# Experts' rows weighted on chip and added by scatter to a copy of y in DRAM, residual kept in SBUF, expert weights loaded per tile, experts and combine in one block

## What is computed

```python
h = x; acc = x                                  # x is the layer-normed input
for _ in range(3):
    h = _l2_normalize(_spmm(vals, row, col, h, n_nodes))
    acc = acc + h
x1 = x_in + acc / 4
y = layernorm(x1)
gate_logits = y @ gate_w + gate_b
topk_vals, topk_idx = jax.lax.top_k(gate_logits, 2)
topk_w = softmax(topk_vals)
h = relu(einsum('bsh,ehf->bsef', y, w1) + b1)   # H=256, F=512, E=16
expert_out = einsum('bsef,efh->bseh', h, w2) + b2
z = y + sum(topk_w[..., None] * selected(expert_out))
out = x1 + layernorm(z) * gamma + beta
```

## Time and profile before

| what | us |
|---|---|
| median of 3 runs (lowest, highest) | 1509.21 (1508.99, 1516.28) |
| the profiled execution's own time | 1510.28 |
| its span, first to last instruction | 1508.6 |
| PE busy in the span | 1294.8 (86%) |
| DVE busy | 1113.5 (74%) |
| ACT busy | 883.1 (59%) |
| POOL busy | 248.7 (16%) |

### The profile page before, as it was taken

One profiled execution on the slowest core, in us unless ns is written; L12 is line 12 of the kernel. 1 busy time (PEld: TensorE's weight loads), 2 busy tenths in 40 slices (PEclk: granted clock), 3 DMA queues, 4 the chain that ended last, 5 costly groups with the idle time before them and its releaser, 6 DMA issues. The chain is left out here.

```text
span 1508.6 us, 31442 instructions
## 1 busy us (share of the span) xinstructions
PE 1294.8 (86%) x9378; PEld 1110.7 (74%) x9379; DVE 1113.5 (74%) x1946; ACT 883.1 (59%) x1937; POOL 248.7 (16%) x233
## 2 busy tenths in 40 slices
PE   4588888888799999999999999999977799999800
PEld 1466666767588888888888888888853799999800
DVE  8888989999676656766655766655567688998768
ACT  1678888888755555655555655555341566666522
POOL 1400000000040000000000000000031578887600
PEclk8799999999999999999999999999986899999955
DMA  5088888888886666656666656666322787334384
GB/s 186 28 207 196 201 199 197 203 202 209 216 233 208 184 184 180 194 170 189 182 189 184 190 164 185 178 189 182 113 91 89 238 272 218 108 105 106 89 289 143
DMA packets 225441, 267.36 MB, mean 177 GB/s; under 512 B 15763, under 2 KB 168066, under 8 KB 225298
## 3 DMA queue, kind: packets, MB, share of 16 engines
q1 hardware_dynamic: 211932, 240.41, 58.0%
q0 software_dynamic: 7680, 20.98, 4.8%
q10 hardware_dynamic: 5760, 5.25, 1.4%
HBM read 175.51 MB, written 91.07 MB: 177 GB/s over the span
## 5 line engine op out<-in xcount | busy, mean ns | idle before, releaser
L844 PE MATMUL ps_rows<-h_both,a_high 128*128 (+1 forms) x1875 | 506.2, 398 | 10.5 <-ACT halves L592 5.3
L684 DVE TENSOR_TENSOR a_low<-a_raw,a_high 128x640 fp32r<-128x640 f32 x375 | 305.6, 823 | 233.7 <-ACT a_high L578 230.4
L578 ACT ACTIVATE a_high<-a_raw 128x640 fp32r<-128x640 f32 x375 | 274.6, 740 | 287.6 <-PE ps_rows L847 265.6
L844 PEld LDWEIGHTS ps_rows<-h_both,a_high 128*128 128x128 f32 x1875 | 330.2, 191 | 68.6 <-ACT halves L592 14.4
L847 PEld LDWEIGHTS ps_rows<-h_both,a_low 128*128 128x128 f32 x1875 | 276.1, 191 | 32.9
L847 PE MATMUL ps_rows<-h_both,a_low 128*128 (+1 forms) x1875 | 284.9, 283 | 0.0
L821 PEld LDWEIGHTS ps_w<-lo_hot,key_w 128*128 128x128 bf16 x2736 | 196.1, 98 | 85.2 <-issue 83.9
L821 PE MATMUL ps_w<-lo_hot,key_w 128*128 128x160 bf16 x2736 | 211.4, 234 | 48.1 <-issue 38.0
L560 ACT ACTIVATE win<-ps_w 128x480 f32<-128x480 f32 x304 | 148.8, 575 | 56.3 <-PE ps_w L826 32.6
L668 DVE TENSOR_TENSOR key_w<-key_hot,tab_marks 128x1536 bf16<-128x1536 bf16 (+1 forms) x228 | 173.8, 817 | 0.0
L551 ACT ACTIVATE key_w<-key_hot,third_b 128x128 bf16<-128x128 bf16 x456 | 144.8, 428 | 5.6 <-DVE key_hot L659 3.1
(11 more groups left out here) (233 smaller groups left out, 1627.4 us busy)
## 6 DMA issues: line engine op xcount, KB each, us to landing
a_raw<-a_rows SPq DMA_DIRECT2D x375, 320.0 KB, 3.2
a_rows<-win SPq DMA_DIRECT2D x228, 240.0 KB, 3.6
w_raw<-in_L_ffn_w SPq DMA_DIRECT2D x32, 512.0 KB
a_rows<-win SPq DMA_DIRECT2D x76, 180.0 KB
b_t<-in_L_ffn_b ACTq DMA_DIRECT2D x40, 128.0 KB, 3.4
hf<-in_x SPq DMA_DIRECT2D x1, 3072.0 KB
x<-in_x SPq DMA_DIRECT2D x1, 3072.0 KB
tokens<-hf SPq DMA_DIRECT2D x4, 768.0 KB
```

The source lines that it names most:

```text
L578: a.activation(a_high[:, u, :], a_raw[:, u, :], ACT.Copy).then_inc(high_split, 1)
L684: v.tensor_tensor(a_low[:, u, :], a_raw[:, u, :], a_high[:, u, :].bitcast(F32), ALU.subtract).then_inc(low_split, 1)
L844: nc.tensor.matmul(ps[:, banks[w][r], :], a_high[:, u, r * P:(r + 1) * P], both, start=first, stop=False, skip_group_check=True)
```

## The change

Five things change together.

1. The shares are no longer kept in SBUF. A row of `tokens` becomes 258 floats wide; the last two are the node's shares, stored by SP in phase_route with 8 bytes a row. The gather brings them along. A new table `pick` says whether a slot is the first or second choice. In the experts' phase DVE makes the slot's weight `w_t` from both (two small operations a tile), and ACT, at the end of its run(t), multiplies `y_t` of tile t-1 by it (`weigh`, two halves).
2. The DRAM tensor `results` gives way to `sums` (`z_dram`). Phase_route stores y there as well; the scatter adds to it during the DMA (`compute_op=ALU.add`). Since a row can be hit by two tiles, each tile's scatter waits until that of the tile before has landed (`z_added`). Combine reads only `sums`.
3. `x1` and `hf` stay in SBUF to the end. The addition of beta moves from POOL in phase_route to POOL in the experts' phase, one chunk after each of 25 scatters. The store and load of `x1_beta` go away.
4. SP loads w1 and w2 for each tile into two buffers each (2 x 512 KB a tile, 40 tiles, where there were 16 experts), and b2 as well, which ACT issued before. For each it reads the expert's number from SBUF. The gathered rows have four buffers, gathers run six tiles ahead of the scatter in POOL's program.
5. Experts and combine share one block, so the engines don't meet between them; combine has five groups instead of seven.

```diff
@@ phase_route
-            full, tail = rows_of(x1_dram, s)
-            sp.wait_ge(beta_added, s.FULL)
-            sp.dma_start(full, x1[:, 0:s.FULL, :]).then_inc(y_stored, 16)
...
+            sp.dma_start(z_full, y[:, 0:s.FULL, :]).then_inc(y_stored, 16)
+            sp.dma_start(z_tail, y[0:s.REST, s.FULL, :]).then_inc(y_stored, 16)
+            full, tail = rows_of(y_dram[:, D:D + 2], s)
+            sp.wait_ge(shares_ready, 2)
+            sp.dma_start(full, shares[:, 0:s.FULL, :]).then_inc(y_stored, 16)
...
-            for c in range(CH):
-                g.tensor_tensor(x1[:, c, :], x1[:, c, :], bt[:], ALU.add).then_inc(beta_added, 1)
@@ phase_experts, SP
+            if late(t, 2):
+                sp.wait_ge(w_low_ready[n], t - 1)
+            sp.dma_start(w_raw[n][:, u, :].rearrange("p (k f) -> p k f", f=dram.shape[2]),
+                         dram[e, :, :].rearrange("a (k p) f -> p (a k) f", p=P)).then_inc(w_loaded[n][u], 16)
@@ phase_experts, POOL
+        def scatter(t):
+            pool.wait_ge(y_ready, (t + 1) * HALVES)
+            if t:
+                pool.wait_ge(z_added, 16 * HALVES * t)
+            for h in range(HALVES):
+                g.indirect_dma_start(
+                    out=z_dram, out_offset=bass.IndirectOffsetOnAxis(
+                        ap=routes.row[:, t * HALVES + h:t * HALVES + h + 1], axis=0),
+                    in_=y_t[:, t % 2, h, :], in_offset=None, compute_op=ALU.add,
+                ).then_inc(z_added, 16)
@@ phase_experts, ACT
+        def weigh(t, u, q):
+            for h in range(HALVES):
+                act.wait_ge(biased, t * HALVES + (h + 1))
+                a.activation(y_t[:, u, h, :], y_t[:, u, h, :], ACT.Copy,
+                             scale=w_t[:, q, h:h + 1]).then_inc(y_ready, 1)
@@ phase_experts, DVE
+        def shares(t, q):
...
+            v.tensor_tensor(share[:, q, :, :], x_t[:, q, :, D:D + 2], routes.pick[:, at, :],
+                            ALU.mult).then_inc(share_ready, 1)
+            dve.wait_ge(share_ready, t + 1)
+            v.tensor_tensor(w_t[:, q, :], share[:, q, :, 0], share[:, q, :, 1], ALU.add).then_inc(share_added, 1)
@@ phase_combine
-        cuts = [0, 2, 6, 11, 16, 20, 23, CH]
+    cuts = [0, 3, 8, 15, 21, CH]
...
+        sp.wait_ge(z_added, s.MT * 16 * (s.TB // P))
```

More of the change, by code:

```diff
@@ L898, in phase_route @@
         den = sb("den", [P, CH])
+        shares = sb("shares", [P, CH, 2])
         choice = sb("choice", [P, 2, CH])
@@ L962, in _ @@
             sp.dma_start(gb[:, :], gate_b.rearrange("(a e) -> a e", a=1).broadcast_to([P, E])).then_inc(consts_in, 16)
[L963 removed]
             sp.dma_start(b1_sb[:, :], b1).then_inc(consts_in, 16)
[L966 removed]
+            full, tail = rows_of(y_dram[:, 0:D], s)
+            z_full, z_tail = rows_of(z_dram[0:s.N, :], s)
             G = s.FULL // 4
@@ L1083, in _ @@
             link(v.tensor_scalar(den[:], ex[:], 1.0, None, ALU.add))
-            link(v.reciprocal(routes.weight[:, 0, :], den[:]))
-            link(v.tensor_tensor(routes.weight[:, 1, :], ex[:], routes.weight[:, 0, :], ALU.mult))
+            v.reciprocal(shares[:, :, 0], den[:]).then_inc(shares_ready, 1)
+            dve.wait_ge(shares_ready, 1)
+            v.tensor_tensor(shares[:, :, 1], ex[:], shares[:, :, 0], ALU.mult).then_inc(shares_ready, 1)
             dve.wait_ge(counted, 1)
@@ L1226, in sb @@
             return ctx.enter_context(nc.sbuf_tensor(name, shape, dt))
-        self.weight = sb("r_weight", [P, 2, s.CH])
+        self.pick = sb("r_pick", [P, s.MT * s.TB // P, 2])
         self.token = sb("r_token", [P, s.MT * s.TB // P], U32)
@@ L1721, in program @@
             y = hf
-            phase_route(nc, s, consts, moments, x1, y, gate_w, gate_b, b1, beta, routes, y_dram, x1_dram)
-        phase_experts(nc, s, routes, w1, w2, b2, y_dram, moe_dram)
-        phase_combine(nc, s, routes, gamma, x1_dram, y_dram, moe_dram, out)
+            phase_route(nc, s, consts, moments, x1, y, gate_w, gate_b, b1, routes, y_dram, z_dram)
+        z = hf
+        with ExitStack() as tail, nc.Block() as block:
+            x1_ready, z_added = phase_experts(nc, s, tail, block, routes, x1, w1, w2, b2, beta, y_dram, z_dram)
+            phase_combine(nc, s, tail, block, x1, z, gamma, z_dram, out, x1_ready, z_added)
 NAMES = ["x", "src", "dst", "edge_weight", "L0_ffn_gate_w", "L0_ffn_gate_b", "L0_ffn_w1", "L0_ffn_b1",
```

778 lines of the change are left out of this document (380 added, 398 removed).

## The result

| | before | changed |
|---|---|---|
| median of 4 runs each (lowest, highest), us | 1511.9 (1508.99, 1516.28) | 1586.01 (1584.48, 1590.81) |
| span of the profiled execution, us | 1508.6 | 1582.7 |

The ratio is 1.0495, 95% interval 1.0465 to 1.0525: the change costs 5%. The forecast was 1532 us with a range up to 1582. The sign was right; the time lies 4 us above the range.

What follows compares the result with a forecast made beforehand. PE was taken to bound the experts' phase (6.15 us a tile) and DVE combine. Route -5.3, experts +56 and combine -28.7 gave +22.0 us, on 1510.28 us 1532.3, forecast as 1532; range 1514 to 1582.

Steps and rivals of the forecast that it cites:

- Route: Routing phase: `gap` no longer held by POOL's 25 additions, 5.5 us saved, `pick` adds 0.25; sum -5.3 us.
- The loop of ACT and DVE: Experts' phase: ACT's `weigh` waits for DVE's `y_t`, nothing overlapped; 7.59 us a tile, taken as 7.7, +56 us.
- The 0.1 us for holds on DVE: Experts' phase: allowance per tile for holds on DVE, such as register work or the 25 additions, raising 7.59 to 7.7 us.
- the rival of the serial scatters: Experts' phase: scatters waiting for one another set the pace, up to 9.0 us a tile, 1543 to 1585 us; chance 0.27.
- POOL: Experts' phase: two gathers, two scatters and one addition take POOL 6.2 to 7 us a tile, under 7.7.
- The clock: Experts' phase: PE's granted clock stays at 2.4 GHz (1.00) although PE idles 1.5 of 7.7 us a tile.
- Combine: Combine with its handoff: fewer DVE additions, waits and groups cut DVE's stretch from 58.8 to 33.6 us; 28.7 us saved altogether.
- The handoff: Between experts and combine: from the last `y_t` to DVE's start in combine, 11.9 us instead of 15.4.
- Tables and layers: Phases ahead of routing: not touched by the change, so they cost what they did.

Runs made afterwards that it cites:

- The experiment in the kernel before: The kernel before, with only ACT's multiplication of y_t by a column of ones added behind DVE's addition of b2, weights resident: 1597.34 us.

## Why the prediction was right and wrong

**Route: right.** -5.3 forecast, -5.5 measured, by the mechanism named: `gap` held by POOL's additions.

**The loop of ACT and DVE: right, and hidden.** 7.59 us by the sum, 7.37 in the run without adding, 7.4 to 7.5 in the changed kernel's first tiles. The gap is `weigh`: from its start to the next `w_high` are 0.82 us (1305.33 to 1306.15), not 1.04; the other terms came within 0.04 us. The 0.1 us for holds on DVE was not needed. The experiment in the kernel before showed a term that the sum would have needed there (ACT's own reading of the expert's number), and that fell away by luck of part (4).

**The step that failed: the rival of the serial scatters, in its second term.** The prediction set its period to L + 1.3, with L = 4.9 + x and x from 0 to 2.8, and chose x = 1.4, "hence the two loops are nearly even". Measured: L = 6.9 from the second issue in the turn shown, x = 2.0, inside its bounds. But the way from the landing to the next tile's second issue is 0.74 + 1.93 = 2.67 us and not 1.3. The 1.3 was the distance of two plain issues; it left out the time from landing to first issue, and that an adding issue takes POOL 1.63 us instead of 1.00. With x = 2.0 and 2.67 the sum is 9.57, the turn in the timeline. Even with the middle x = 1.4 the right second term gives 9.0, well above 7.7, and this rival would have been the forecast: 37 tiles at 9.0 give about 1580. The mechanism was named, with its sign; its size and so its rank were wrong. An unknown price was bounded for the landing and not for the issue, and one unknown was taken at its middle where the forecast hung on it.

**POOL: wrong, without effect on the time.** 8.31 us of own work (in the run without the wait), not 6.2 to 7; the prediction's own terms add up to 7.4 at their upper end. It lies under 9.43, so the changed kernel doesn't show it; both runs that shorten the adding scatters' loop, by its wait or by the weights' load, met it first. The bounds, in order: PE 6.15, ACT with DVE 7.37, POOL 8.33, adding scatters 9.43.

**The clock: forecast 1.00, granted 0.89,** with stretches at 1.2 GHz (0.50) from 1223 us on. PE was busy 16.59 of 20 us from 1200 to 1220 us, at 1.00, and 15.79 of 20 from 1240 to 1260, at 0.84. That it costs time is shown nowhere: PE waits 36.2 us in 175 for `hid`, so it has room, and the chain of the scatters has no PE in it. At 7.4 us a tile the clock was 1.00 (run without adding), at 8.33 it was 0.91, at 8.5 (ACT in the loop of the kernel before) 0.90, at 9.4 0.88.

**Combine: mechanism right, size off by 7.** DVE's stretch is 35.4 us (1542.39 to 1577.83) where 33.6 were forecast, and the last store takes 4.9 instead of 4.1. The handoff is 16.05 us instead of 11.9: the sum let the last scatter go as soon as `weigh` was done (1527.71), but it stood until 1533.28 for the landing of the scatter before, 5.6 us. The load behind it was faster than forecast, 3.4 against 4.9.

**Tables and layers: forecast 0, measured -11.0,** cause open. Without it the changed kernel would be at 1597, and further from the forecast.

**The range.** It ended at 1582 because the serial rival was priced at 9.0 us at most. Its bound for landing held; the sum around it didn't.

## What to carry to other kernels

A wait for a DMA's landing between iterations makes a loop of everything from issue to issue: count the issues on the queue's engine, the landing under the load of that moment, and the reaction after it, and bound each of them when the operation is new. Before work is moved to "an idle engine", add up that engine's per-iteration time with its gaps, and ask what shares its path to SBUF; and look for waits in the program of the loading engine that stand ahead of a load which doesn't need them. When the bound is taken away the next one is often a microsecond below: an experiment for each, on its own, tells which part of a large change is worth keeping.

## What the runs showed of the hardware

- An indirect scatter that adds f32 rows of 1 KB in DRAM: 1.63 us a 128-row issue on POOL against 1.00, 5.7 us median to landing against 3.9 beside the same loads, 4.7 with light ones. It also costs DMA time: at the same share of 0.75 the adding scatters' kernel moved 184 GB/s, the same kernel with plain scatters 229.
- Trainium skill, "DMA: Bandwidth & Descriptors", section "Anatomy of one DMA — SWDGE (gpsimd) path": 2.0 us plus bytes at 436 GB/s, an estimate of 2.3 us for 128 KB. Beside the weights' loads no landing came near it: 3.9 plain, 5.7 adding. With the weights in and DMA at a share of 0.25 it did: plain scatters took 2.4 us (median of 48, in the run with ACT in the loop of the kernel before).
- A POOL `tensor_tensor` of 128x256 f32 took 0.68 us in phase_route, 0.8 beside DVE's combine, and in the experts' phase 1.0 (run without adding), 1.3 (changed kernel) and 1.7 (run without the wait), all beside a DVE busy for 66 to 83% of the time; one DVE operation of 25 elements beside it went from 0.2 to 5.7 us, small ones from 0.16 to 0.65.
- Where ACT's program reads two numbers from SBUF for an address, ACT stood idle for 0.7 to 1.0 us, with "issue" as the end of it; that the reading is the cause is inferred from the program's order.
